# Wider attention products, paired LayerNorm statistics and single-copy normalised tiles in a vision tower on one core

## The chip, the cores and the metric

The kernel runs on one core of a Trainium2 chip. The metric is device time in microseconds (us) from start to end of one execution, and the median of several executions counts. The core has five engines with queues of their own: TensorE (PE, with its weight loads shown apart as PEld), VectorE (DVE), ScalarE (ACT), GpSimd (POOL) and SyncE (SP), which only issues transfers. They meet through semaphores.

## The reference

1,024 tokens of 192 features go through five blocks; all of it is computed in one launch.

1. Tokenizer: 960 pixel values per token, LayerNorm, a product to 192 features.
2. Masked attention, 12 heads of 16 features, 64 sequences of 16 tokens: `out = softmax(q k^T / 4 + mask) v`, projected and added.
3. A mixture of 8 experts of 288 hidden units, the two best kept for each token.
4. A block of the RWKV kind: two LayerNorms in a row, a recurrence forward and backward, an output product, a second normalised feed-forward part (768 units, squared ReLU) with a gate.
5. Attention again, with a gated low-rank addition to q, k and v from 8 experts.

Each of the five phases starts with `(x - mean(x)) * rsqrt(var(x) + eps)` over the 192 features of each token.

## The kernel before

**Layout.** Tokens lie in 8 tiles of 128 (token on the partition). The residual stream is `H` (128 x 8 x 192, float32), the stream inside block 4 is `Z`. Products need features on the partitions, so each normalised tile is written to `xn` and turned by TensorE into a PSUM bank. ACT then writes the float16 high part `X_hi` and DVE the remainder `X_lo` (`x_low`), and every product of the kernel is made of float16 high and low parts. Features 128 to 191 are needed twice, at partitions 0 to 63 and again at 64 to 127.

**LayerNorm of one tile** (`ln_stats`, line 1010; `one_over_std`, line 505; `ln_norm`, line 1016). DVE runs `bn_stats` (line 1011), waits for it by a semaphore, runs `bn_aggr` (line 1012). POOL adds epsilon (line 508), waits for itself, and raises to the power -0.5 (line 511). DVE writes `xn` in two instructions: 192 columns (line 1021), then columns 128 to 191 a second time beside them (line 1024). TensorE turns the 256 columns with two float32 transposes per tile (`turn`, line 1572), two tiles to a bank, and the last one releases ACT.

**The order of LayerNorm work.** `norm_tiles` (line 1032) handles four tiles: statistics of tile t, then `ln_norm` of tile t-1, so each tile's root runs on POOL while DVE works on the next tile. It is called six times: tiles 0 to 3 and 4 to 7 before the experts (`moe`), before the feed-forward part of block 4 (`mix2`), and before the second attention (`attn1`). Block 4's two LayerNorms in a row are `norm_twice` (line 1045), with a root for H, a normalisation to Z (line 1053), and a root for Z per tile. Tiles 0 to 3 of it are spread over expert steps 9 to 14; tiles 4 to 7 come in one piece when the experts are done. The first attention's tiles (`attn0`) call `ln_stats` and `ln_norm` one by one in the tokenizer's loop (lines 1299 to 1308).

**Attention** (`attention`, lines 724, 1091, 1609). Two halves of 512 tokens, hf 0 and 1, are interleaved by a list of steps, `ATTENTION_ORDER`: ... `pt` 0, `ot` 0, `st` 1, `pj` 0, `values0` 1, `s` 1, `values1` 1, `pt` 1, `ot` 1, `pj` 1. `st` (`scores`, line 1630) forms for each of 32 groups of 16 tokens (g) a product of a block-diagonal key matrix (made by DVE's `spread`, line 1108) with 16 tokens' queries: for high and low parts one product of 2 x 16 columns and one of 16, times two row sets of 128 and 64 features. That is 128 products a half, in 4 banks. `ot` (`outputs`, line 1694) does the same with values and probabilities. DVE sums each bank's two column sets (line 1143). `pj` is the output projection, 24 products of 192 columns. `values0/1` are 128 float16 transposes a half which ACT (lines 732, 738) and DVE (line 1139) copy out. `s` and `pt` turn scores and probabilities.

**Planned banks.** Every use of a PSUM bank is planned in `plan_fills`: it names the previous user whose release TensorE waits for. SP issues the next weight transfer when POOL has finished the low parts (`low_part`, line 513) of the weights before.

## Time and profile before

| | |
|---|---|
| median of 3 runs | 509.55 us (505.12, 509.55, 509.74) |
| the profiled execution | 506.86 us, span 505.1 us |
| mean granted TensorE clock | 0.78 of full speed |
| PE / PEld busy | 344.7 us (68%) / 257.1 us (51%) |
| DVE busy | 412.2 us (82%), 896 instructions |
| ACT / POOL busy | 227.3 us (45%) / 144.7 us (29%) |
| tokenizer | 0 to 62 us |
| first attention | 62 to 150 us |
| experts | 144 to 250 us |
| block 4: double LayerNorm, recurrence, feed-forward | 250 to 394 us |
| second attention with its gates | 389 to 505 us |

Busy time says how long an engine held an instruction, not whether anyone waited for it. The chain of waits follows the last instruction back to what released it, so it names the engine that set the time in each stretch. A granted clock of 1.00 is 2.4 GHz, 0.50 is 1.2 GHz.

### The profile page before, as it was taken

The numbers are of one execution on the slowest core, as the hardware profiler recorded it, in microseconds if no ns is written. First come the engines' busy times: TensorE is split into PE (matmuls) and PEld (weight loads), VectorE is DVE, ScalarE is ACT, GpSimd is POOL, SyncE is SP. The second block draws the span as 40 slices with busy tenths as digits, with TensorE's granted clock in tenths as the row PEclk, the third lists the DMA queues.
The fourth block names the chain that finished last, engine by engine and source line by source line (L and its number), as shares of the span: only waits on it lengthen the run. The fifth ranks groups of instructions, "written<-read, shape, count | busy, mean of one in ns | idle before, by whom it ended". The sixth has DMA issues, their size and how long they took to land.

```text
span 505.1 us, 8830 instructions
## 1 busy us (share of the span) xinstructions
PE 344.7 (68%) x3474; PEld 257.1 (51%) x3474; DVE 412.2 (82%) x896; ACT 227.3 (45%) x391; POOL 144.7 (29%) x194
## 2 busy tenths in 40 slices
PE   4766649897769899999926000006799268798976
PEld 4665619596646567776702000004359125655955
DVE  3799998998886654887779999998899869776974
ACT  4566383718375796644315660000084122363171
POOL 3535252042430433242042469811301120000000
PEclk9979986959577999999968555555599668578586
DMA  7635000030050002000000000000000000000000
GB/s 275 228 106 228 2 1 1 1 143 1 2 215 1 2 0 95 2 1 1 0 2 1 0 0 0 0 1 0 2 0 1 1 1 1 1 2 1 2 34 31
DMA packets 4235, 17.51 MB, mean 35 GB/s; under 512 B 857, under 2 KB 1762, under 8 KB 3682
## 3 DMA queue, kind: packets, MB, share of 16 engines
q1 hardware_dynamic: 4194, 16.95, 9.2%
q8 instruction: 27, 0.44, 0.4%
q14 instruction: 14, 0.11, 0.1%
HBM read 16.16 MB, written 0.79 MB: 34 GB/s over the span
## 4 chain that ended last, share of the span: by engine, by line
DVE 46%; PE 34%; ACT 8%; issue 6%; POOL 4%; DMA 1%; SPq 0%; DVEq 0%; POOLq 0%; ACTq 0%
PE PS L1527 30%; DVE R L1108 4%; DVE R L1378 3%; DVE R L1380 3%; POOL rstd L511 3%; DVE R L1432 2%; DVE Q L1098 2%; PE PS L1659 2%; DVE R L1001 1%; DVE stats L1011 1%; DMA T<-tok_w 1%; DVE xn L1021 1%; DVE stats L964 1%; POOL ve L508 1%; PE PS L1666 1%
## 5 line engine op out<-in xcount | busy, mean ns | idle before, releaser
L1527 PE MATMUL PS<-late_a,Q 128*128 128x192 f16 x48 | 9.9, 360 | 72.0 <-DVE Q L1435 70.3
L508 POOL TENSOR_SCALAR ve<-mv 128x1 f32<-128x1 f32 x56 | 14.4, 257 | 149.9 <-DVE mv L1012 131.1
L1527 PE MATMUL PS<-Q,R 128*128 128x32 f16 (+3 forms) x1024 | 46.4, 192 | 14.0 <-DVE R L1108 9.7
L1527 PE MATMUL PS<-m,Q 128*128 128x192 f16 (+1 forms) x576 | 51.9, 245 | 2.4 <-DVE Q L1324 2.4
L1527 PEld LDWEIGHTS PS<-Q,R 64*64 64x64 f16 (+1 forms) x1024 | 44.6, 125 | 17.2 <-DVE R L1108 10.2
L1527 PEld LDWEIGHTS PS<-m,Q 128*128 128x128 f16 (+1 forms) x576 | 45.8, 96 | 11.8 <-issue 8.0
L1527 PEld LDWEIGHTS PS<-late_a,Q 128*128 128x128 f16 x48 | 6.2, 139 | 73.8 <-issue 73.4
L1324 DVE TENSOR_TENSOR Q<-Q 128x512 f16<-128x512 f32 x36 | 26.5, 751 | 19.2 <-ACT Q L813 19.0
L1527 PE MATMUL PS<-X_hi,R 128*128 128x512 f16 x144 | 41.2, 392 | 0.0
L808 ACT ACTIVATE Q<-PS,col 128x512 f32<-128x512 f32 x36 | 24.8, 689 | 28.9 <-PE PS L1527 28.8
L1108 DVE TENSOR_SCALAR R<-Q,K 128x1024 f16<-128x1024 f16 x80 | 37.3, 539 | 0.3
L1527 PE MATMUL PS<-X_hi,late_a 128*128 128x512 f16 (+1 forms) x72 | 30.4, 445 | 10.1 <-DVE X_hi L1088 5.6
L511 POOL TENSOR_TENSOR rstd<-ve,mhalf 128x1 f32<-128x1 f32 x56 | 33.6, 600 | 4.7
L1339 DVE SCALAR_TENSOR_TENSOR H<-PS,gat,H 128x192 f32<-128x192 f32 x64 | 23.2, 411 | 5.8 <-PE PS L1527 4.8
L1582 PE MATMUL PS<-K,xn 128*128 128x128 f32 x80 | 16.3, 324 | 13.6 <-DVE xn L1024 13.5
L1527 PE MATMUL PS<-R 128*128 128x192 f16 x184 | 17.8, 257 | 10.8 <-DVE R L981 10.8
L1527 PE MATMUL PS<-X_hi,late_b 128*128 128x512 f16 (+1 forms) x72 | 25.2, 431 | 0.0
L813 ACT ACTIVATE Q<-PS,col 128x512 f16<-128x512 f32 x36 | 24.9, 690 | 0.0
L732 ACT ACTIVATE R<-PS 128x1024 f16<-128x1024 f16 x16 | 15.6, 1015 | 19.7 <-PE PS L1659 19.7
L1143 DVE TENSOR_REDUCE Q<-PS 128x128 f32<-128x256 f32 x64 | 22.1, 408 | 2.8 <-PE PS L1527 2.7
L516 POOL TENSOR_TENSOR R<-T,R 128x576 f16<-128x576 f32 x8 | 15.7, 1989 | 26.7 <-ACT T L712 26.7
L1527 PEld LDWEIGHTS PS<-X_hi,R 128*128 128x128 f16 x144 | 14.4, 100 | 16.5 <-issue 2.2
(233 smaller groups left out, 932.3 us busy)
## 6 DMA issues: line engine op xcount, KB each, us to landing
R<-tok_x SPq DMA_DIRECT2D x8, 480.0 KB, 3.6
T<-tok_w SPq DMA_DIRECT2D x6, 480.0 KB, 7.3
T<-late SPq DMA_DIRECT2D x1, 2632.0 KB, 8.7
T<-moe SPq DMA_DIRECT2D x1, 2304.0 KB, 8.8
T<-moe SPq DMA_DIRECT2D x1, 1728.0 KB, 8.0
T<-full SPq DMA_DIRECT2D x1, 1152.0 KB, 5.3
R<-early SPq DMA_DIRECT2D x1, 776.0 KB, 9.8
out<-H SPq DMA_DIRECT2D x4, 192.0 KB, 1.9
```

The costliest lines, as they stand in the source:

```text
L508: nc.gpsimd.tensor_scalar(ve[:, t:t + 1], mv[:, t, 1:2], EPS, None, ALU.add).then_inc(pool_step, 1)
L511: nc.gpsimd.tensor_tensor(rstd[:, t:t + 1], ve[:, t:t + 1], mhalf[:], ALU.pow).then_inc(rstd_ready, 1)
L516: nc.gpsimd.tensor_tensor(lo, raw, hi, ALU.subtract).then_inc(wlo, 1)
L732: nc.scalar.activation(VA[:, hl, 8 * g:8 * g + 8, :], bank(name).bitcast(F16).rearrange("p (s n) -> p s n", s=8), ACT.Copy).then_inc(v_act ...
L808: nc.scalar.activation(ge[n % 3], bank(("h", n)), ACT.Gelu, bias=b, scale=1.0 / WS).then_inc(act_step, 1)
L813: nc.scalar.activation(hgh[slot], bank(("h", n)), ACT.Gelu, bias=b, scale=1.0 / WS).then_inc(gelu_ready, 1)
L1108: ins = V.tensor_scalar(v[:, :, :, h], w, K[:, mask + h:mask + h + 1], None, ALU.mult)
L1143: return V.tensor_reduce(dst, src.rearrange("p (l n) -> p n l", l=2), AX, ALU.add)
L1324: V.tensor_tensor(hgl[slot], ge[n % 3], hgh[slot], ALU.subtract).then_inc(hp_ready, 1)
L1339: ins = V.scalar_tensor_tensor(H[:, t], bank(name)[:, C * j:C * j + C], gat[:, 5, t, e:e + 1], H[:, t], ALU.mult, ALU.add)
L1527: return T_.matmul(o, w, x, start=start, stop=stop, skip_group_check=True)
L1582: last = T_.transpose(bank(name)[:, 256 * j + P * k:256 * j + P * k + P], xn[:, t % 4, P * k:P * k + P], ident)
```

## The change

LayerNorm statistics are taken for two tiles at a time and POOL raises a 128 x 2 operand instead of 128 x 1; in `norm_tiles` both pairs' statistics come first and the four normalisations after them; `norm_twice` spreads as pairs over the same six steps. The first attention's tiles keep `ln_stats`. `xn` holds 192 columns, written once; each tile is turned by a transpose of columns 0 to 127 and one of columns 64 to 191, and columns 128 to 191 are turned a third time into partitions 0 to 63 of the second, over the part of it that is not wanted. In `st` of half 1 and `ot` of half 0, group s writes up to 3 groups of 16 columns (times 2 for high and low) in its first product and up to 6 in its second. The columns beyond its own 16 are overwritten by the next group, whose first product starts afresh. `ot` of half 1 and `st` of half 0 keep their 32 and 16 columns.

```diff
@@ -502,13 +502,13 @@
             nc.gpsimd.memset(ones[:], 1.0).then_inc(const_ready, 1)
             steps = [0]
 
-            def one_over_std(n, t):
+            def one_over_std(n, t, w=1):
 
                 pool.wait_ge(var_ready, n + 1)
-                nc.gpsimd.tensor_scalar(ve[:, t:t + 1], mv[:, t, 1:2], EPS, None, ALU.add).then_inc(pool_step, 1)
+                nc.gpsimd.tensor_scalar(ve[:, t:t + w], mv[:, t:t + w, 1], EPS, None, ALU.add).then_inc(pool_step, 1)
                 steps[0] += 1
                 pool.wait_ge(pool_step, steps[0])
-                nc.gpsimd.tensor_tensor(rstd[:, t:t + 1], ve[:, t:t + 1], mhalf[:], ALU.pow).then_inc(rstd_ready, 1)
+                nc.gpsimd.tensor_tensor(rstd[:, t:t + w], ve[:, t:t + w], mhalf[:, 0:w], ALU.pow).then_inc(rstd_ready, 1)
 
             def low_part(n, raw, hi, lo):
 
@@ -578,12 +578,9 @@
             pool.wait_ge(wlo, NM + NL + 1)
 
             for hf in range(2):
-                for k in range(5):
-                    if k:
-                        one_over_std(n, 4 * hf + k - 1)
-                        n += 1
-                    if k < 4:
-                        one_over_std(n, 4 * hf + k)
+                for _ in ("H", "Z"):
+                    for t in (4 * hf, 4 * hf + 2):
+                        one_over_std(n, t, 2)
                         n += 1
 
             def link(ins):
@@ -1013,15 +1010,22 @@
                 nn[0] += 1
                 return nn[0]
 
+            def ln_stats_pair(t, src):
+                c = 6 * (t // 2 % 2)
+                sa, sc = stats[:, 0, c:c + 6], stats[:, 1, c:c + 6]
+                V.bn_stats(sa, src[:, t])
+                link(V.bn_stats(sc, src[:, t + 1]))
+                V.bn_aggr(mv[:, t], sa)
+                V.bn_aggr(mv[:, t + 1], sc).then_inc(var_ready, 1)
+                nn[0] += 1
+                return nn[0]
+
             def ln_norm(t, src, n, k):
 
                 dve.wait_ge(rstd_ready, n)
                 if k >= 4:
                     dve.wait_ge(psum_filled, x_fill(k - 4))
-                V.tensor_scalar(xn[:, t % 4, 0:C], src[:, t], mv[:, t, 0:1], rstd[:, t:t + 1], ALU.subtract,
-                                ALU.mult).then_inc(dve_step, 1)
-                chain[0] += 1
-                V.tensor_scalar(xn[:, t % 4, C:2 * P], src[:, t, P:C], mv[:, t, 0:1], rstd[:, t:t + 1], ALU.subtract,
+                V.tensor_scalar(xn[:, t % 4], src[:, t], mv[:, t, 0:1], rstd[:, t:t + 1], ALU.subtract,
                                 ALU.mult).then_inc(xn_ready, 1)
 
             def x_fill(k):
@@ -1031,29 +1035,30 @@
 
             def norm_tiles(src, ready=None, tiles=range(NT)):
 
-                last = None
-                for t in range(tiles[0], tiles[-1] + 2):
-                    if t in tiles:
-                        if ready:
-                            ready(t)
-                        now = ln_stats(t, src)
-                    if last:
-                        ln_norm(t - 1, src, last, xc[0])
+                seen = []
+                for t in range(tiles[0], tiles[-1], 2):
+                    if ready:
+                        ready(t)
+                    seen.append(ln_stats_pair(t, src))
+                for t in tiles:
+                    ln_norm(t, src, seen[(t - tiles[0]) // 2], xc[0])
+                    xc[0] += 1
+
+            def norm_twice(hf, k):
+
+                t = 4 * hf + 2 * (k % 2)
+                if k < 2:
+                    first[t] = ln_stats_pair(t, H)
+                elif k < 4:
+                    dve.wait_ge(rstd_ready, first[t])
+                    V.tensor_scalar(Z[:, t], H[:, t], mv[:, t, 0:1], rstd[:, t:t + 1], ALU.subtract, ALU.mult)
+                    link(V.tensor_scalar(Z[:, t + 1], H[:, t + 1], mv[:, t + 1, 0:1], rstd[:, t + 1:t + 2],
+                                         ALU.subtract, ALU.mult))
+                    second[t] = ln_stats_pair(t, Z)
+                else:
+                    for i in range(2):
+                        ln_norm(t + i, Z, second[t], xc[0])
                         xc[0] += 1
-                    last = now
-
-            def norm_twice(hf, k):
-
-                if k >= 2:
-                    ln_norm(4 * hf + k - 2, Z, second[k - 2], xc[0])
-                    xc[0] += 1
-                if 1 <= k < 5:
-                    t = 4 * hf + k - 1
-                    dve.wait_ge(rstd_ready, first[k - 1])
-                    link(V.tensor_scalar(Z[:, t], H[:, t], mv[:, t, 0:1], rstd[:, t:t + 1], ALU.subtract, ALU.mult))
-                    second[k - 1] = ln_stats(t, Z)
-                if k < 4:
-                    first[k] = ln_stats(4 * hf + k, H)
             first, second = {}, {}
 
             def x_low(phase, pairs_=range(4)):
@@ -1574,13 +1579,15 @@
                 for pr in pairs_:
                     name = ("x", phase, pr)
                     free(name)
+                    x = xn[:, 2 * pr % 4:2 * pr % 4 + 2]
+                    o = bank(name).rearrange("p (j k n) -> p j k n", j=2, k=2)
                     for j in range(2):
                         xc[0] += 1
                         pe.wait_ge(xn_ready, xc[0])
-                        t = 2 * pr + j
-                        for k in range(2):
-                            last = T_.transpose(bank(name)[:, 256 * j + P * k:256 * j + P * k + P],
-                                                xn[:, t % 4, P * k:P * k + P], ident)
+                        T_.transpose(o[:, j, 0], x[:, j, 0:P], ident)
+                        T_.transpose(o[:, j, 1], x[:, j, CB:C], ident)
+                    for j in range(2):
+                        last = T_.transpose(o[0:CB, j, 1], x[:, j, P:C], ident)
                     last.then_inc(psum_filled, 1)
 
             def by_rows(o, wa, wb, col0, m, hf, more=()):
@@ -1627,26 +1634,33 @@
                             more = ((bh, hw_hi[:, sl]), (bh, hw_lo[:, sl]), (bl, hw_hi[:, sl]), (bb, cstack[0:72, sl]))
                         by_rows(bank(name)[0:m], wa, wb, c0 + o, m, hf, more).then_inc(psum_filled, 1)
 
+                def columns(g, s, images):
+                    n = 16 * min(images, 8 - s)
+                    return slice(16 * g, 16 * g + n), slice(16 * s, 16 * s + n)
+
                 def scores(hf):
 
                     n0 = 2 * a + hf
                     pe.wait_ge(bd_ready, 3 * n0 + 2)
                     pe.wait_ge(qkv_ready, 5 * n0 + 5)
                     qa, qb = pairs["QA"], pairs["QB"]
+                    near, far = (3, 6) if hf == 1 else (1, 1)
                     for t in range(4):
                         name = ("st", a, hf, t)
                         free(name)
                         oa, ob = (bank(name)[:, 2 * P * k:2 * P * (k + 1)].rearrange("p (l n) -> p l n", l=2) for k in range(2))
                         for s in range(8):
                             g = 8 * t + s
-                            q, o = slice(16 * g, 16 * g + 16), slice(16 * s, 16 * s + 16)
+                            q, o = columns(g, s, near)
+                            ql, ol = columns(g, s, far)
                             mm(oa[:, :, o], KAbd[:, 0, g], qa[:, :, q], True, False)
-                            mm(oa[:, 0, o], KAbd[:, 1, g], qa[:, 0, q], False, True)
+                            mm(oa[:, 0, ol], KAbd[:, 1, g], qa[:, 0, ql], False, True)
                         for s in range(8):
                             g = 8 * t + s
-                            q, o = slice(16 * g, 16 * g + 16), slice(16 * s, 16 * s + 16)
+                            q, o = columns(g, s, near)
+                            ql, ol = columns(g, s, far)
                             mm(ob[0:CB, :, o], KVBbd[0:CB, 0, g], qb[0:CB, :, q], True, False)
-                            last = mm(ob[0:CB, 0, o], KVBbd[0:CB, 1, g], qb[0:CB, 0, q], False, True)
+                            last = mm(ob[0:CB, 0, ol], KVBbd[0:CB, 1, g], qb[0:CB, 0, ql], False, True)
                         last.then_inc(psum_filled, 1)
 
                 def values(hf, hl):
...
```

(POOL's other calls of `one_over_std` go over even tiles with width 2 in the same way; `outputs` gets the same edit as `scores`, with `columns(s, s, near)` on the probabilities and `near, far = (3, 6) if hf == 0 else (1, 1)`; `mhalf` grows from [P, 1] to [P, 2], `xn` from [P, 4, 256] to [P, 4, 192].)

## Rows read from the trace of the kernel before

**Rows 1.** The page's chain that ended last, by engine
```profile
DVE 46%; PE 34%; ACT 8%; issue 6%; POOL 4%; DMA 1%; SPq 0%; DVEq 0%; POOLq 0%; ACTq 0%
```

**Rows 2.** Windows: stretch, then busy us (and instructions) of each engine, granted clock, DMA
```profile
50.00:60.00 10.00, 5.84 (x65) 5.44 (x64) 9.60 (x28) 4.06 (x7) 2.90 (x8) 1.00 0.00 1
170.00:244.00 74.00, 72.76 (x619) 52.13 (x619) 49.97 (x119) 46.54 (x81) 24.20 (x29) 1.00 0.05 17
```

**Rows 3.** Timeline of DVE, one norm_tiles call: start us, duration us, instruction, [idle before]
```profile
389.15 0.36 DVE L1011 BATCH_NORM_STATS2 stats<-H 128x6 f32<-128x192 f32 x1
389.54 0.18 DVE L1012 BATCH_NORM_AGGREGATE mv<-stats 128x2 f32<-128x6 f32 x1
389.64 0.33 DVE L1011 BATCH_NORM_STATS2 stats<-H 128x6 f32<-128x192 f32 x1
...
390.72 0.38 DVE L1021 TENSOR_SCALAR xn<-H,mv,rstd 128x192 f32<-128x192 f32 x1 [0.54 <-POOL rstd L511]
391.02 0.31 DVE L1024 TENSOR_SCALAR xn<-H,mv,rstd 128x64 f32<-128x64 f32 x1
391.24 0.35 DVE L1011 BATCH_NORM_STATS2 stats<-H 128x6 f32<-128x192 f32 x1
...
394.31 0.55 DVE L1473 SCALAR_TENSOR_TENSOR R<-R,PS 128x384 f32<-128x384 f32 x1
```

**Rows 4.** Timeline of POOL beside it, the first two roots
```profile
389.81 0.22 POOL L508 TENSOR_SCALAR ve<-mv 128x1 f32<-128x1 f32 x1 [24.76 <-DVE mv L1012]
390.12 0.57 POOL L511 TENSOR_TENSOR rstd<-ve,mhalf 128x1 f32<-128x1 f32 x1
390.66 0.22 POOL L508 TENSOR_SCALAR ve<-mv 128x1 f32<-128x1 f32 x1
```

**Rows 5.** Timeline of POOL and DVE, the end of the experts' first norm_tiles
```profile
133.67 2.52 POOL L516 TENSOR_TENSOR m<-T,m 128x576 f16<-128x576 f32 x2
...
133.74 1.32 DVE L1021 TENSOR_SCALAR xn<-H,mv,rstd 128x192 f32<-128x192 f32 x1 [0.34 <-POOL rstd L511]
134.99 1.26 DVE L1024 TENSOR_SCALAR xn<-H,mv,rstd 128x64 f32<-128x64 f32 x1
```

**Rows 6.** Timeline of DVE, first instruction of norm_twice and the first behind it
```profile
250.10 0.36 DVE L1011 BATCH_NORM_STATS2 stats<-H 128x6 f32<-128x192 f32 x1
...
262.70 0.54 DVE L1076 TENSOR_SCALAR R<-PS,col 128x256 f32<-128x256 f32 x1
```

**Rows 7.** Timeline of PE: transposes at either clock, products of 192 columns
```profile
353.81 1.80 PE L1582 MATMUL PS<-K,xn 128*128 128x128 f32 x6
355.80 0.69 PE L1582 MATMUL PS<-K,xn 128*128 128x128 f32 x2 [0.19 <-DVE xn L1024]
...
365.42 1.04 PE L1582 MATMUL PS<-K,xn 128*128 128x128 f32 x8
...
385.61 6.10 PE L1527 MATMUL PS<-fullp,R 128*128 128x192 f16 x72
```

**Rows 8.** Timeline of DVE, two waits behind a norm_tiles call
```profile
366.06 0.55 DVE L1076 TENSOR_SCALAR R<-PS,col 128x256 f32<-128x256 f32 x1 [0.37 <-PE PS L1582]
...
418.26 0.75 DVE L1098 SCALAR_TENSOR_TENSOR Q<-PS,col,Q 128x512 f16<-128x512 f32 x1 [0.82 <-ACT Q L752]
```

**Rows 9.** Timeline of PE: st of half 1, first attention; ot and st, second
```profile
105.04 5.99 PE L1527 MATMUL PS<-Q,R 128*128 128x32 f16 x128 [0.17 <-DVE R L1108]
...
462.92 11.49 PE L1527 MATMUL PS<-Q,R 128*128 128x32 f16 x256 [1.28 <-DVE Q L1163]
```

**Rows 10.** Windows of line 1527 alone in ot and st: PE, PEld, clock, DMA
```profile
99.72:101.72 2.00, 2.00 (x62) 1.93 (x63) 1.00 0.00 0
...
470.00:472.00 2.00, 2.00 (x50) 1.93 (x50) 0.50 0.03 8
```

**Rows 11.** Timeline of DVE: the softmax of half 1, first and second attention
```profile
119.12 0.56 DVE L1118 SCALAR_TENSOR_TENSOR Q<-PS,K 128x384 f32<-128x384 f32 x1 [1.52 <-PE PS L1677]
...
481.75 0.56 DVE L1121 TENSOR_SCALAR Q<-PS 128x384 f32<-128x384 f32 x1 [0.72 <-PE PS L1677]
```

More of the change, by code:

```diff
@@ L250, in build @@
         id16 = sb("id16", [P, P], F16)
-        mhalf = sb("mhalf", [P, 1])
+        mhalf = sb("mhalf", [P, 2])
         tokb = sb("tokb", [P, C])
@@ L258, in build @@
         rstd = sb("rstd", [P, NT])
-        xn = sb("xn", [P, NT // 2, 2 * P])
+        xn = sb("xn", [P, NT // 2, C])
         X_hi = sb("X_hi", [P, NT, 2, P], F16)
@@ L564, in _ @@
                 if i == 11:
-                    for t in range(4):
-                        one_over_std(n, t)
+                    for t in (0, 2):
+                        one_over_std(n, t, 2)
                         n += 1
                 low_part(i, raw, hi, lo)
-            for t in range(4, NT):
-                one_over_std(n, t)
+            for t in (4, 6):
+                one_over_std(n, t, 2)
                 n += 1
@@ L580, in _ @@
             for hf in range(2):
-                for k in range(5):
-                    if k:
-                        one_over_std(n, 4 * hf + k - 1)
-                        n += 1
-                    if k < 4:
-                        one_over_std(n, 4 * hf + k)
+                for _ in ("H", "Z"):
+                    for t in (4 * hf, 4 * hf + 2):
+                        one_over_std(n, t, 2)
                         n += 1
@@ L629, in _ @@
             for phase in range(2):
-                for t in range(NT):
-                    one_over_std(n, t)
+                for t in range(0, NT, 2):
+                    one_over_std(n, t, 2)
                     n += 1
@@ L1697, in outputs @@
                     pe.wait_ge(v_dve_ready, 4 * (n0 + 1))
+                    near, far = (3, 6) if hf == 0 else (1, 1)
                     for t in range(4):
@@ L1704, in outputs @@
                             g = 8 * t + s
-                            q = o = slice(16 * s, 16 * s + 16)
+                            q, o = columns(s, s, near)
+                            ql, ol = columns(s, s, far)
                             mm(oa[:, :, o], VA[:, 0, g], PT[:, :, t, 0, q], True, False)
-                            mm(oa[:, 0, o], VA[:, 1, g], PT[:, 0, t, 0, q], False, True)
+                            mm(oa[:, 0, ol], VA[:, 1, g], PT[:, 0, t, 0, ql], False, True)
                         for s in range(8):
                             g = 8 * t + s
-                            q = o = slice(16 * s, 16 * s + 16)
+                            q, o = columns(s, s, near)
+                            ql, ol = columns(s, s, far)
                             mm(ob[0:CB, :, o], VB[0:CB, 0, g], PT[0:CB, :, t, 1, q], True, False)
-                            last = mm(ob[0:CB, 0, o], VB[0:CB, 1, g], PT[0:CB, 0, t, 1, q], False, True)
+                            last = mm(ob[0:CB, 0, ol], VB[0:CB, 1, g], PT[0:CB, 0, t, 1, ql], False, True)
                         last.then_inc(psum_filled, 1)
```

## The prediction

> **What bounds the kernel.** I read the chain of waits first: DVE sets the end for 46% of the span and PE for 34%, POOL alone for 4% [rows 1]. So no engine is the bound throughout, and each edit has to be priced in its own stretch. The windows say which: in the tokenizer DVE works 96% of the time; in the 74 us of the experts PE works 98% at full clock with DVE at 50 of 74 us [rows 2], so LayerNorm work there costs nothing unless it lies on PE. The timelines of the LayerNorm calls come next. One call for four tiles takes 389.15 to 394.31 = 5.16 us on DVE, with waits for POOL's root in it, and nothing else is on DVE meanwhile [rows 3]. The double LayerNorm of block 4 takes 12.60 us for four tiles [rows 6]. Last, the attention: st of half 1 waits only for DVE's spread at 105.04 [rows 9], and DVE waits behind it for 1.52 us in the first attention and 0.72 in the second [rows 11]. That wait bounds what faster products can give.
>
> **LayerNorm, one call of four tiles.** From the rows: bn_aggr starts 0.39 us after its bn_stats, the next bn_stats 0.10 later; a 192-column xn write takes 0.30 start to start, the second write 0.22 [rows 3]. POOL's epsilon starts 0.27 after bn_aggr, the root 0.31 later, the root takes 0.57, and the next epsilon may start 0.03 before it ends [rows 4]. DVE starts 0.03 after the root. I take 0.26 for two bn_stats in a row (0.33 less the overlap seen between unlinked instructions). New call, from zero: bn_stats 0 and 0.26, bn_aggr 0.65 and 0.75, second pair 0.85 to 1.60; first root 1.33 to 1.90; second epsilon 1.87, root 2.18 to 2.75; xn at 1.94, 2.24, 2.78, 3.08, next work at 3.38. That is 5.16 - 3.38 = 1.78 us less a call, of which 4 x 0.22 are the dropped writes and the rest waits.
>
> **The root of two columns** is nowhere in the trace. It isn't cheaper than one (0.57), and at most it is double (1.14). Between them I take 0.75: of the 0.57, 0.22 is what the plain epsilon takes [rows 4] and only the remaining 0.35 can grow, which caps it near 0.92; 0.75 is the middle. Then the call ends at 3.74 and saves 1.42 us (at 1.14: it ends at 4.52 and saves 0.64).
>
> **Which calls are on the path.** Six calls:
> - Experts, tiles 0 to 3: DVE goes straight on. Two xn writes run into POOL's weight low parts and take 1.32 and 1.26 us instead of 0.38 and 0.31 [rows 5]. POOL again starts these as soon as its last root is out, so I keep the collision: two writes meet it, as before. Saves 1.4.
> - Experts, tiles 4 to 7: x_low behind it waits for the last transposes, which now are four after the last xn instead of two. At full clock a transpose is (1.04 - 0.27)/7 = 0.11 us [rows 7], so 0.2 is given back. Saves 1.2.
> - mix2, tiles 0 to 3: PE works at half clock there, and pair 0's transposes can't start before the output products end at 353.81. A transpose costs 0.69 - 0.48 = 0.21 us at that clock [rows 7]; twelve instead of eight add 0.8, which eats what the earlier xn gives. Mix2, tiles 4 to 7: DVE already waits 0.37 us for PE's transposes, which stand behind three key products [rows 8]. The xn come 1.4 us earlier for nothing and four transposes more cost 0.4. Both together: -0.4.
> - attn1, tiles 0 to 3: the feed-forward output of tiles 4 to 7 is ready on PE at 391.7, before DVE gets to it. Saves 1.4.
> - attn1, tiles 4 to 7: after it DVE waits 0.82 us for ACT and PE's second qkv slot [rows 8]; PE is the limit. The wait grows by what the call gives. 0.
>
> **The double LayerNorm, tiles 4 to 7.** Same steps: both pairs of H statistics 0 to 1.78; roots ready at 2.08 and 3.11; Z of pair 0, its statistics to about 3.8; Z of pair 1, its statistics to about 5.3; roots of Z out at 4.8 and 6.4; last xn at about 6.8, next work at 7.1. x_affine of pair 1 then waits some 0.35 for four transposes at half clock. 12.60 - 7.45 = **5.15 us** (5.5 at 0.57, 4.1 at 1.14). It is the largest term: per tile a root of H and a root of Z were waited for one after the other, four times; now it is twice each with the other pair between. All of it is on the path, since nothing else runs on DVE and the recurrence behind it needs the same engine.
>
> **Tokenizer.** Eight second writes of 0.22 go; DVE has 96% there, ACT sometimes ends the wait. I count 1.5 of the 1.76. **Transposes inside the experts:** the mix1 turn sits in PE's full stretch; four more x 0.11 = 0.4 lost. Elsewhere the extra transposes lie in PE's idle time.
>
> **The 96-column products.** What the rows show: at full clock a 24-column product (mean of 32 and 16) comes every 2.00/62 = 32 ns, at half clock every 2.00/50 = 40 (45 over the whole 256, which take 11.49 us) [rows 9, 10]. PE is busy throughout both windows, and yet the clock, 1.00 in the first two us of `ot`, is 0.50 well inside it. 72 products of 192 columns take (6.10 - 0.17)/72 = 82 ns each [rows 7], that is 2.4 columns per ns plus 2.4 ns, and 619 such wide instructions hold 1.00 for 74 us [rows 2]. The new products have 96 columns down to 16 at the end of each bank: mean 75. At full clock, by the larger of 32 ns and columns/2.4 + 3, that is 39 ns each, 5.0 us a half-step instead of 5.2 to 6.0; at half clock 65 ns, 8.3 us. I take the full clock: streaming then fills 0.8 of the time, against 0.3 now, nearer to the rows that hold it than to those that lose it. Gain, first attention: st starts at 105.04 with the spread as before [rows 9], ends at 110.0 instead of 111.0, and the 24 products of the projection run at full clock, 2 us instead of 4. PE is then 3 us ahead and the value transposes wait for DVE's spread, so the gain is at most DVE's 1.52 us wait [rows 11]. ACT, which copies values out and weights before them without a pause, passes on about half: 0.85. In the second attention ACT has no weights to split; there DVE's 0.72 goes whole [rows 11], with two pauses of 0.15 ahead of it: 1.05. The 0.85 goes unchanged into the experts' first call, since there DVE follows at once. Together 1.9.
>
> The Trainium skill (TensorE: Matmul & The Clock Gate, section Back-to-back issue gap) says that a stream of weight load and matmul pairs settles at about 81 ns a product at 128 columns. The trace disagrees: 82 ns is its figure for 192 columns, not for 128 [rows 7]. By the page 256 products would take an estimated 20.7 us and the kernel would end near 515, where the last rival ends too.
>
> **Sum.** 1.5 + 1.4 + 1.2 - 0.4 (mix1 turn) + 5.15 - 0.4 (mix2) + 1.4 + 1.9 = 11.75 us. From the profiled execution of 506.86: 495.1. The median before is 2.7 above the profile, and two of three runs lie there; by it, 497.8. I say **496**. With the root at 0.57 it is 1.5 less, with 1.14 it is 3.4 more.
>
> **Rivals.**
> 1. *The root of two costs twice one.* 0.57 to 1.14: 506.86 - 8.4 = 498.5. For it: 0.35 of the 0.57 is work beyond an add.
> 2. *The gain comes back in a queue.* PE or ACT stands behind one of the calls I count in full, as it does in mix2; with attn1 and one experts' call gone and half of the attention's 1.9: 506.86 - 8 = 499 to 501. For it: PE is busy in every stretch after a call but one.
> 3. *The clock falls all the same.* Full clock for the first 2 us, then 65 ns each: 51 products in the 2 us and 205 x 0.065 = 13.3 make 15.3 us for 256, against 11.3 now (5.2 + 6.0 in the first attention, 11.5 in the second), in both attentions. That is 8 lost instead of 1.9 won: 506.86 - 9.85 + 8 = 505, within 1%. Against it: the fill of 0.8.
> 4. *Slower: each wide product takes about 80 ns*, as 96 columns would at half clock throughout with nothing overlapped. 256 of them take 20.5 us instead of 11.3, in both attentions, and DVE waits for all of it: +18.2 - 9.85 gives 515. It decides from (11.3 + 9.85/2) us for 256, or 63 ns each, upward. Against it: 82 ns at 192 columns [rows 7].
>
> **Chances.** The forecast 0.72, rival 1 0.08, rival 2 0.08, rival 3 0.08, rival 4 0.04. A measurement of this kernel tells about 1% (5 us) from nothing. Rivals 1 and 2 are faster by more than that except for some 0.02; with rival 3 that makes 0.10 for within 1%, 0.04 slower, 0.86 faster. Range: the low end is the root at 0.57 and both mix2 and the second attn1 call giving 1.5 each, 506.86 - 16 = 491; the high end takes in rivals 1 and 2 on the basis of the median, 502.
>
> **What would show it.** In the page after: granted clock 1.00 or near in `ot` 0 and `st` 1, 39 ns a product; no L1024 group; 36 roots on POOL instead of 56; the root's mean, 0.57 to 1.14; each LayerNorm call 3.4 to 3.8 us; double LayerNorm near 7; in mix2 longer waits of DVE for PE. I am wrong if the two-column root is above 1.2 us, if the clock is 0.5 in the wide products, or if DVE's new waits behind the calls sum to more than 5 us.

## The result, and the profile after

| | before | after |
|---|---|---|
| median | 508.07 us (505.12 to 509.74, 20 runs) | 502.39 us (494.00 to 505.06, 20 runs) |
| profiled execution, span | 506.86, 505.1 | 504.28, 502.4 |
| PE / DVE / POOL busy | 344.7 / 412.2 / 144.7 us | 358.6 / 399.7 / 129.7 us |
| DVE instructions | 896 | 856 |
| mean granted clock | 0.78 | 0.784 |

The executions of the changed kernel fall into two groups: 9 of 20 at 494.0 to 497.4 us, with a mean clock of 0.80 to 0.81, and 11 at 502.4 to 505.1, at 0.78. The kernel before has one group. The comparison leaves out runs that lie over 1.5% above the fastest of their kernel (here and in every ratio below), so its ratio of 0.9756 (95% interval 0.9732 to 0.9779) is that of the lower group; the medians of all runs stand as 0.989, a gain of 5.7 us. The forecast of 496 is the lower group (mean 495.4), the mean of the upper is 503.7, and the profile shown here is one of the upper group. So there are two questions: do the steps hold, and what are the 8 us between the groups?

The chain of waits by engine in the page after, beside [rows 1]: DVE and POOL, where the LayerNorm part works, have less, PE 6 points more.

```profile
DVE 41%; PE 40%; ACT 9%; issue 6%; POOL 2%; DMA 1%; SPq 0%; DVEq 0%; POOLq 0%; ACTq 0%
```

**LayerNorm.** DVE's timeline of the call that [rows 3] show (start us, duration us, instruction, idle before and releaser):

```profile
388.31 0.36 DVE L1016 BATCH_NORM_STATS2 stats<-H 128x6 f32<-128x192 f32 x1
...
390.35 0.67 DVE L1028 TENSOR_SCALAR xn<-H,mv,rstd 128x192 f32<-128x192 f32 x2 [0.35 <-POOL rstd L511]
391.34 0.67 DVE L1028 TENSOR_SCALAR xn<-H,mv,rstd 128x192 f32<-128x192 f32 x2 [0.32 <-POOL rstd L511]
391.92 0.55 DVE L1478 SCALAR_TENSOR_TENSOR R<-R,PS 128x384 f32<-128x384 f32 x1
```

From the first bn_stats to the next work it is 3.61 us (forecast 3.74, before 5.16). What remains are two waits for POOL, one a pair. On POOL the root of two columns takes 0.71 us, and the next pair's epsilon starts before it ends:

```profile
256.28 0.22 POOL L508 TENSOR_SCALAR ve<-mv 128x2 f32<-128x2 f32 x1 [20.08 <-DVE mv L1019]
256.59 0.71 POOL L511 TENSOR_TENSOR rstd<-ve,mhalf 128x2 f32<-128x2 f32 x1
257.27 0.22 POOL L508 TENSOR_SCALAR ve<-mv 128x2 f32<-128x2 f32 x1
```

The double LayerNorm of tiles 4 to 7, DVE, beside [rows 6]: 255.30 to 262.18 = 6.88 us, with 0.50 of a new wait for PE's transposes behind it (forecast 7.1 and 0.35, before 12.60).

```profile
255.30 0.36 DVE L1016 BATCH_NORM_STATS2 stats<-H 128x6 f32<-128x192 f32 x1
...
260.34 0.64 DVE L1028 TENSOR_SCALAR xn<-T,mv,rstd 128x192 f32<-128x192 f32 x2
261.60 0.67 DVE L1028 TENSOR_SCALAR xn<-T,mv,rstd 128x192 f32<-128x192 f32 x2 [0.61 <-POOL rstd L511]
262.18 0.54 DVE L1081 TENSOR_SCALAR R<-PS,col 128x256 f32<-128x256 f32 x1
...
263.67 0.54 DVE L1081 TENSOR_SCALAR R<-PS,col 128x256 f32<-128x256 f32 x1 [0.50 <-PE PS L1590]
```

**The wide products.** PE's timeline of `ot` 0 and `st` 1, 256 products in one row, in the first and the second attention; [rows 9] have the narrow ones. Then PE's windows in the first (stretch, length, PE busy and instructions, granted clock, DMA share and GB/s):

```profile
100.88 18.47 PE L1532 MATMUL PS<-Q,R 128*128 128x96 f16 x256 [2.11 <-DVE Q L1168]
...
460.39 10.99 PE L1532 MATMUL PS<-Q,R 128*128 128x96 f16 x256 [1.28 <-DVE Q L1168]
```

```profile
100.00:101.00 1.00, 0.12 (x3) 1.00 0.00 0
101.00:102.00 1.00, 1.00 (x18) 0.53 0.00 0
102.00:103.00 1.00, 1.00 (x16) 0.50 0.00 0
...
118.00:119.00 1.00, 1.00 (x18) 0.50 0.00 0
...
122.00:123.00 1.00, 1.00 (x19) 1.00 0.00 0
```

The same 256 products take 18.47 us in the first attention and 10.99 in the second. In the first the clock is 1.00 while TensorE waits 2.11 us, and 0.50 right after it starts to work. It stays at 0.50 for 20 us in which PE is busy without a pause, and comes back 2.3 us into the 192-column products behind them. The difference, 7.5 us, is near the 8.3 us between the means of the two groups.

**The ledger by stretch**, each from the start of one instruction of the timelines to the start of the next named, the last one DVE's last residual add; "filled" is the run f1_fill below, whose first attention holds the clock.

| stretch (us) | before | after | filled | forecast gain |
|---|---|---|---|---|
| to the first low part of qkv (tokenizer) | 64.63 | 64.67 | 64.79 | 1.5 |
| to `st` 0 | 11.55 | 12.05 | 12.05 | 0 |
| to `ot` 0 | 23.54 | 24.16 | 23.75 | 0 |
| `ot` 0 and `st` 1, to `pj` 0 | 11.24 | 18.40 | 10.94 | } 0.85 |
| to `ot` 1 | 17.19 | 15.85 | 15.96 | } |
| to the experts' ct transposes (two calls) | 37.44 | 33.89 | 33.94 | 2.6 |
| experts, to the first b2 product | 37.65 | 39.41 | 39.42 | 0 |
| to the last b2 product (mix1 turn) | 44.07 | 44.52 | 44.52 | -0.4 |
| double LayerNorm, to the recurrence | 18.99 | 13.41 | 13.42 | 5.15 |
| recurrence and mix2, to feed-forward | 103.35 | 102.46 | 102.46 | -0.4 |
| to the second attention's gates | 30.68 | 29.11 | 29.09 | 1.4 |
| to `ot` 0 of the second attention | 62.59 | 62.46 | 62.44 | 0 |
| to the last residual add | 39.27 | 39.09 | 39.09 | 1.05 |

The columns after and filled differ by 7.6 us, 7.46 of it in one line.

### The profile page after: what moved, and what is told of

The parts are those of the page before. It is cut to its first block, busy times and chain, and to the rows that moved or that the text cites. A ratio compares the mean times of both kernels' runs of the same rounds, so it can differ in the third digit from the quotient of the medians.

```text
span 502.4 us, 8830 instructions
## 1 busy us (share of the span) xinstructions
PE 358.6 (71%) x3514; PEld 272.6 (54%) x3514; DVE 399.7 (80%) x856; ACT 227.7 (45%) x391; POOL 129.7 (26%) x154
## 4 chain that ended last, share of the span: by engine, by line
DVE 41%; PE 40%; ACT 9%; issue 6%; POOL 2%; DMA 1%; SPq 0%; DVEq 0%; POOLq 0%; ACTq 0%
PE PS L1532 34%; DVE R L1383 3%; DVE R L1385 3%; DVE R L1113 3%; DVE R L1437 2%; DVE Q L1103 2%; PE PS L1673 2%; DVE R L998 1%; DMA T<-tok_w 1%; POOL rstd L511 1%; PE PS L1680 1%; DVE stats L961 1%; ACT Q L886 1%; DVE R L1397 1%; DVE smx L1128 1%
## 5 line engine op out<-in xcount | busy, mean ns | idle before, releaser
L1532 PE MATMUL PS<-Q,R 128*128 128x96 f16 (+9 forms) x1024 | 52.0, 208 | 13.1 <-DVE R L1113 8.9
L1532 PEld LDWEIGHTS PS<-Q,R 64*64 64x64 f16 (+1 forms) x1024 | 50.3, 124 | 16.3 <-DVE R L1113 9.3
L1532 PE MATMUL PS<-m,Q 128*128 128x192 f16 (+1 forms) x576 | 53.5, 249 | 3.0 <-ACT Q L822 2.4
L1532 PEld LDWEIGHTS PS<-m,Q 128*128 128x128 f16 (+1 forms) x576 | 47.2, 98 | 12.3 <-issue 6.9
L508 POOL TENSOR_SCALAR ve<-mv 128x2 f32<-128x2 f32 (+1 forms) x36 | 8.6, 238 | 160.9 <-DVE mv L1019 133.4
L1532 PE MATMUL PS<-X_hi,R 128*128 128x512 f16 x144 | 39.6, 380 | 0.0
L1532 PE MATMUL PS<-R 128*128 128x192 f16 x184 | 20.6, 280 | 8.5 <-DVE R L978 8.5
L511 POOL TENSOR_TENSOR rstd<-ve,mhalf 128x2 f32<-128x2 f32 (+1 forms) x36 | 24.3, 675 | 3.0
L1532 PEld LDWEIGHTS PS<-R 128*128 128x128 f16 x184 | 18.3, 112 | 10.1 <-DVE R L978 9.7
L862 ACT ACTIVATE Q<-R 128x512 f16<-128x512 f32 x3 | 1.9, 629 | 46.4 <-DVE R L1438 46.4
## 6 DMA issues: line engine op xcount, KB each, us to landing
R<-early SPq DMA_DIRECT2D x1, 776.0 KB, 10.3
```

The costliest lines, as they stand in the source:

```text
L511: nc.gpsimd.tensor_tensor(rstd[:, t:t + w], ve[:, t:t + w], mhalf[:, 0:w], ALU.pow).then_inc(rstd_ready, 1)
L1532: return T_.matmul(o, w, x, start=start, stop=stop, skip_group_check=True)
```

## The experiments

Twelve kernels, in three sets of four; those of a set ran on one chip beside the kernel before, most of them 6 times (e3 8, g1 12). Theory A: the wide products keep a full clock that they find and don't bring back a lost one, and the 2.1 us idle ahead of `ot` 0 is where it is lost. Theory B: the groups come from elsewhere.

**Which part makes the groups.** Four runs: the changed kernel again; its LayerNorm part alone; the wide products alone on the kernel before; everything, with wide products in the second attention only.

```diff
 e2_ln_only (both places):
-                    near, far = (3, 6) if hf == 1 else (1, 1)
+                    near, far = 1, 1
 e4_wide_second:
+                    near, far = (3, 6) if a == 1 and hf == 1 else (1, 1)
```

> The changed kernel once more, unchanged. In its profile the clock stood at 0.50 through `ot` 0 and `st` 1 of the first attention (256 products in 18.5 us) and at 1.00 in the second attention. Theory A: wide products keep a full clock that they find, but don't bring one back; whether they find it after PE's 2.1 us of idle ahead of `ot` 0 differs from execution to execution. Then executions fall into two groups some 8 us apart, near 495 and 503, and a profile of the lower group shows about 10 us for the 256 products. Theory B: the two groups come from another stretch (tokenizer, experts), and the 256 products take about 18 us in both.

> The LayerNorm part alone (pairs, single copy, three transposes); all attention products narrow as in the kernel before. Theory A: one group of executions, 8 to 10 us under the kernel before (ratio 0.981 to 0.984), by the LayerNorm terms read from the profile of after: about 1.5, 1, 5.1, 0.9, 1.5 us. Theory B: two groups 8 us apart here too.

> The kernel before with the wide products alone. Theory A: two groups, one about 2 us under the kernel before (as forecast: 0.85 + 1.05), one some 5 to 7 us above it. Theory B: one group, within 2 us of the kernel before.

> The changed kernel with wide products in the second attention only; the first attention's are narrow. Theory A: the slow group is gone; all executions lie at 496 to 498, since the second attention held its clock in the profile of after, and its gain of 1 us stays. Theory B: still two groups 8 us apart.

| | median us (range) | ratio to before, 95% |
|---|---|---|
| before | 507.49 | |
| e1_after_again | 503.35 (495.1; five at 502.5 to 504.4) | 0.983, 0.976 to 0.990 |
| e2_ln_only | 499.75 (498.2 to 504.5) | 0.986, 0.983 to 0.990 |
| e3_wide_only | 510.16 (508.9 to 511.2, one 515.0) | 1.006, 1.004 to 1.009 |
| e4_wide_second | 499.44 (495.7 to 501.2) | 0.983, 0.979 to 0.987 |

Without wide products in the first attention (e2, e4) nothing lies above 501.2 but one run of 504.5; with them (e1) five of six do. So the groups seem to come with the wide products of the first attention. The LayerNorm part gives 7.7 us in the median, a little less than the 8 to 10 expected, and e4 lies above the 496 to 498 expected. The profile of e4 shows something more: narrow products, and the clock lost at their start all the same.

```profile
98.36 11.89 PE L1532 MATMUL PS<-Q,R 128*128 128x32 f16 x256 [2.11 <-DVE Q L1168]
```

```profile
99.00:100.00 1.00, 1.00 (x22) 0.50 0.00 0
```

From `ot` 0 to `pj` 0 it needs 11.8 us, and the kernel before, which loses the clock only within `ot` 0, 11.2. So the loss needs no wide products, and with narrow ones it costs 0.6 us instead of 7.5. But e3 goes against the simple form of A and fits neither of its two groups: with the same wait of 2.11 us ahead of it, its stream holds the full clock, and yet the kernel is slower than before. First PE's `ot` 0 of e3, then its windows in the experts:

```profile
99.13 10.99 PE L1527 MATMUL PS<-Q,R 128*128 128x96 f16 x256 [2.11 <-DVE Q L1163]
```

```profile
166.00:168.00 2.00, 1.40 (x7) 1.00 0.01 4
168.00:170.00 2.00, 0.15 (x2) 0.99 0.00 0
170.00:172.00 2.00, 2.00 (x14) 0.50 0.00 0
172.00:174.00 2.00, 2.00 (x15) 0.50 0.00 0
...
176.00:178.00 2.00, 2.00 (x9) 0.80 0.05 8
```

It gains 1.3 us from `ot` 0 to `ot` 1 and loses 3.3 in the experts, behind another wait of TensorE (2.45 us, ahead of the down products of unit 3), and 1.2 in the second attention ahead of `ot` 0. The experts' loss is not a matter of the change: their first stretch took 37.65 us in the profile of before and 39.3 to 40.9 in the five others so far, always behind that wait. An idle of 2 us or more is thus survived at times and not at others.

**Fill the idle.** Added products of 512 columns write a PSUM bank that is free and overwritten later: nine ahead of `ot` 0 (f1), ten more ahead of the experts' unit 3 (f2), and the nine with narrow products throughout (f3).

```diff
+                        if a == 0 and hf == 0 and t == 0:
+                            for _ in range(9):
+                                mm(bank(name), id16[:], wa[:, 0, 0:512], True, True)
                         pe.wait_ge(pt_ready, 2 * n0 + t // 2 + 1)
 f2_fill_both, besides:
+                    if u == 3:
+                        spare = ("h", unit_chunks(u + 1)[0][0])
+                        free(spare)
+                        for _ in range(10):
+                            mm(bank(spare), id16[:], early_a[:, 0, 0:512], True, True)
                     free(("y", v, 0))
```

> The kernel after, with nine added products of 512 columns on TensorE (0.22 us each at full clock, about 1.95 us) that write the still unused PSUM bank of the first `ot` tile, in the 2.1 us in which TensorE waits for VectorE's last pt copy ahead of `ot` 0 of the first attention. Their result is overwritten; nothing else changes. Theory A (the 96-column products keep a full clock they find and do not bring one back; the idle ahead of `ot` 0 is what takes it): the first attention's 256 products take 10.9 us at granted clock 1.00 in every execution, the upper group of times (502 to 505) is gone, and the median lies at 494 to 497. Theory B (the two groups come from elsewhere, or the clock falls by what came earlier): both groups stay and the products still take 18.4 us in the upper one; median 502 to 504. If the added products themselves are late, ot 0 starts later by up to 0.3 us.

> The kernel of the run before (nine added products ahead of `ot` 0) and ten more added products of 512 columns ahead of the down products of the experts' unit 3, where TensorE waits 2.45 us in every profile so far, after which the clock was 1.00 in one profile and 0.50 for 3 to 7 us in the five others. They write the PSUM bank of the next unit's first chunk, which is free there. Theory A: the clock stays at 1.00 in the experts, and the stretch from the ct transposes to the b2 products takes 37.7 us instead of 39.4: 1.5 us under the run before, 493 to 495. Theory B (the clock there does not follow from that idle): no change, or up to 1 us slower where the added products end after the wait.

> The nine added products ahead of `ot` 0, but all attention products 16 and 32 columns wide as in the kernel before (the LayerNorm part of the change stays). If the narrow stream loses the clock by itself, `ot` of the first attention starts at 1.00 and falls to 0.50 within it, as in the profile of before, and the time is that of the kernel with the LayerNorm part alone, 498 to 500. If only the idle ahead of it took the clock, 256 products take 8.2 us (32 ns each) and the time is that of the wide kernel with the added products, 494 to 497: then the width is not needed.

With the kernel before at 508.03: f1 496.38 us (495.1 to 496.7 four times, 500.7 and 501.0), ratio 0.980 (0.976 to 0.984); f2 **491.71** (489.8 to 495.5), ratio 0.971 (0.967 to 0.975); f3 499.23 (495.6 to 505.6), ratio 0.981 (0.978 to 0.984). PE of f1, then of f3:

```profile
98.41 2.11 PE L1532 MATMUL PS<-early_a,id 128*128 128x512 f16 x9
100.59 11.00 PE L1532 MATMUL PS<-Q,R 128*128 128x96 f16 x256
```

```profile
95.94 2.11 PE L1532 MATMUL PS<-early_a,id 128*128 128x512 f16 x9
98.12 4.79 PE L1532 MATMUL PS<-Q,R 128*128 128x32 f16 x128
103.53 5.99 PE L1532 MATMUL PS<-Q,R 128*128 128x32 f16 x128 [0.61 <-DVE R L1113]
```

```profile
98.00:100.00 2.00, 1.93 (x58) 1.00 0.00 0
100.00:102.00 2.00, 2.00 (x62) 0.92 0.03 8
102.00:104.00 2.00, 1.39 (x32) 0.50 0.00 0
```

In f1 the added products end just before the first product of `ot` 0 starts, and 256 wide products take 11.0 us instead of 18.5. In f1, f2 and g4 below, 18 runs, none lies above 501.0 and 16 lie under 497; of the 32 runs of the changed kernel in three sets 21 lie at 501.3 to 505.1. That idle is what costs the upper group its clock. (Some 5 us are lost in some other place as well, which no profile shows: f1 has two runs at 500.7 and 501.0, f2 three at 493.3 to 495.5 beside three at 489.8 to 490.1, and f3, without wide products, two at 505.1 and 505.6, at a mean clock of 0.77 and not the 0.78 of the changed kernel's upper group. So a run's time alone doesn't say which loss it had.) In f3 the narrow stream has the same full clock ahead of it and falls to 0.50 within 4 us: the wide stream keeps a clock that the narrow one loses, as the prediction had it. What that is worth in time is not settled: the medians differ by 2.9 us, with ranges that overlap, but in f3's profile, the fastest of its six, the stretch from `ot` 0 to the ct transposes takes 61.2 us, in f1's 60.8, in e2's (narrow, idle not filled) 63.4. And with ten products in the experts' wait, the stretch to the first b2 product takes 37.75 us instead of 39.4, at 1.00 throughout. PE's windows there, of the changed kernel and of f2:

```profile
174.00:176.00 2.00, 1.22 (x14) 1.00 0.00 0
176.00:178.00 2.00, 2.00 (x16) 0.54 0.04 8
178.00:180.00 2.00, 2.00 (x14) 0.61 0.00 0
```

```profile
164.00:166.00 2.00, 1.72 (x12) 1.00 0.00 0
166.00:168.00 2.00, 2.00 (x26) 1.00 0.03 8
172.00:174.00 2.00, 2.00 (x24) 1.00 0.00 0
```

Over all profiles: 37.6 to 37.8 us in the three kernels with those ten products (f2, g1, g4), 37.65 in one of the eleven without them, 39.3 to 40.9 in ten. The median of f2 lies 4.7 us under that of f1 and under the 493 expected at the lowest, which these 1.7 us don't account for. In its profile 2.3 us more are gained in the second attention ahead of `ot` 0 (60.1 against 62.4) and 1.5 in the tokenizer, where nothing was added; g4, with the same ten products, has 62.4 there.

**Do the added products pay by themselves?** Both stretches of them in the kernel before.

> The kernel BEFORE, with none of the change, and both stretches of added products (nine ahead of `ot` 0 of the first attention, ten ahead of the down products of the experts' unit 3). If the added products are worth something by themselves, whatever the change, it is 1.5 us or more under the kernel before. By theory A they need the wide products to pay in the attention: the narrow stream loses the clock within itself (in the run with added products and narrow columns it fell 3 us in), and in the experts the profile of before showed no loss to win back. So within 1 us of before in its profile, and 0 to 2 us in the median, by how often the experts' clock falls.

506.94 us (12 runs) against 507.55 (17 runs), ratio 1.000 (0.998 to 1.002). They don't. In g1's profile the clock is 1.00 ahead of its narrow products and falls to 0.78 and 0.50 within 4 us of their start, as in f3. What the added products give, they give to the wide stream and to the experts.

**The single write and third transposes.** Undone in f4: two writes and two transposes a tile, as before.

```diff
...
+                V.tensor_scalar(xn[:, t % 4, C:2 * P], src[:, t, P:C], mv[:, t, 0:1], rstd[:, t:t + 1], ALU.subtract,
...
 turn():
+                        for k in range(2):
+                            last = T_.transpose(bank(name)[:, 256 * j + P * k:256 * j + P * k + P],
+                                                xn[:, t % 4, P * k:P * k + P], ident)
```

> The kernel after with the third part of the change undone: each normalised tile is written twice by VectorE (192 columns and the last 64 again) and transposed twice by TensorE instead of written once and transposed three times; pairs with one root each and the 96-column products stay. By the prediction the single write saves 0.22 us a tile where VectorE sets the end (8 tiles of the tokenizer, 4 and 4 of the experts, 4 of the double LayerNorm, 4 of attn1) and the third transpose costs 0.4 us at mix1 and 0.4 at mix2: 24 x 0.22 = 5.3, of which some 1.5 was lost in the tokenizer's clock, less 0.8: 3 to 4.5 us slower than the kernel after in the same group of times, which for the upper group is 506 to 508. The rival that the third transposes eat the gain says no difference (within 1 us).

498.29 us (494.5, 495.7, 496.7, 499.9, 500.9, and 507.7), ratio 0.980 (0.976 to 0.984). Its profile is 500.87, 4.2 above f1's, of which 1.4 is the experts' clock. In the double LayerNorm it needs only 0.27 us more (13.69 against 13.42), where four second writes of 0.22 had been counted. DVE there shows why:

```profile
256.50 0.31 DVE L1031 TENSOR_SCALAR xn<-T,mv,rstd 128x64 f32<-128x64 f32 x1
256.97 0.38 DVE L1028 TENSOR_SCALAR xn<-T,mv,rstd 128x192 f32<-128x192 f32 x1 [0.16 <-POOL rstd L511]
...
258.92 0.53 DVE L1084 TENSOR_SCALAR R<-PS,col 128x256 f32<-128x256 f32 x1
```

The first pair's second writes lie in the wait for the root (0.16 instead of 0.61), and nothing is waited for behind the call, where the third transposes cost 0.50. Against them stand 0.5 us ahead of `st` 0 and 0.44 at mix1, which f4 gets back. Five runs of 494.5 to 500.9 have a mean of 497.5, against 495.4 for the nine of the changed kernel's lower group, but 497.6 for the six of f1, which holds the clock in the same place. So the part is worth 0 to 2 us, not the 3 to 4.5 expected; these few runs don't tell it from nothing. One thing I had not looked for: by their times, 12 of 14 runs with two writes (e3 and f4) are without the 7.5 us, and 15 of 38 with one write (after, e1, g2, g3). The profiles with wide products and the idle left as it is agree, two of two and none of four. The wait is 2.1 us in both, and why the number of writes should matter is not shown.

**Columns and a lost clock; a third place filled.** g2 is the changed kernel once more, g3 has (4, 8) for (3, 6), g4 is f2 with added products ahead of `pt` 1 and `ot` 1 and wide products in `ot` 1 of the first attention too.

```diff
 g4_fill_three, in the turn of the probabilities:
+                        if a == 0 and hf == 1:
+                            for _ in range(1 if pr else 9):
+                                mm(bank(name), id16[:], wa[:, 0, 0:512], True, True)
...
 and in ot:
+                    near, far = (3, 6) if hf == 0 or a == 0 else (1, 1)
```

> The kernel after once more, beside the versions with added products on the same chip. Both theories: two groups of times, 494 to 498 and 502 to 505; theory A says that the version with both stretches of added products (490 to 495.5) lies under both groups.

> The kernel after with 128 columns instead of 96 in the wide products (four images in both parts instead of three, eight instead of six). At full clock 256 of them take (mean 104 columns) 104 / 2.4 + 3 = 46 ns each = 11.9 us, 1 us more than now; the lower group is then 0 to 1 us above that of the kernel after. If more columns bring a lost clock back, the upper group is gone. By theory A (what is lost ahead of `ot` stays lost until the 192-column products of the projection) they run at half clock throughout where it is lost, some 95 ns each = 24 us, and the upper group lies near 508 to 511.

> The version with both stretches of added products, and more of them: nine ahead of the transposes of the probabilities of half 1 of the first attention (TensorE waits 2.3 us there), one and two in the waits behind these, and 96-column products in `ot` of half 1 as well. Now those 256 products run at half clock and narrow, about 11.5 us, and the projection behind them at half clock, 4 us. Theory A: the clock holds, they take 11 us and the projection 2 us; the gain is at most 2.5 us, less what VectorE, which stands behind `ot` here, takes anyway: 0 to 2 us under the version before it, 488 to 494. If the clock falls all the same, 96 columns at half clock cost 18.4 us instead of 11.5: 5 to 7 us slower than it, 496 to 501.

Beside 507.55 for before: g2 502.96 us (495.7; five at 501.3 to 504.3), ratio 0.985 (0.979 to 0.990). g3 497.43 (four at 494.4 to 498.2, two at 506.5 and 506.7, under the 508 to 511 expected), ratio 0.977 (0.974 to 0.981). g4 493.78 (491.9 to 496.6), ratio 0.973 (0.970 to 0.976). PE of g3 in the first and second attention:

```profile
100.30 21.38 PE L1532 MATMUL PS<-Q,R 128*128 128x128 f16 x256 [2.11 <-DVE Q L1168]
...
462.77 12.38 PE L1532 MATMUL PS<-Q,R 128*128 128x128 f16 x256 [1.28 <-DVE Q L1168]
```

128 columns don't bring the clock back either: 0.50 for 21 us. (The expectation put their mean at 104; over both products of a group it is 88, hence 48 ns each at full clock and 84 at half.) g4 can't be told from f2 by the intervals, and the gain of 0 to 2 us expected over it isn't there. Its stretch of `ot` 1 held the clock, but the wait for VectorE behind it grew from 1.41 us in f2 to 2.70, and after the next one the clock was 0.50, where f2 had 1.00:

```profile
125.38 5.54 PE L1532 MATMUL PS<-Q,R 128*128 128x96 f16 x128 [0.43 <-DVE Q L1168]
...
135.08 0.41 PE L1532 MATMUL PS<-early_a,Q 128*128 128x192 f16 x3 [2.70 <-DVE Q L1183]
145.91 0.19 PE L1532 MATMUL PS<-early_a,X_hi 128*128 128x8 f16 x1 [1.94 <-DVE X_hi L1070]
```

```profile
144.00:146.00 2.00, 0.09 (x3) 0.93 0.52 215
146.00:148.00 2.00, 2.00 (x50) 0.50 0.00 0
```

From `ot` 1 to the ct transposes it needs 35.1 us, f2 33.9. So f2 has the lowest median of all: 16.3 us under the kernel before (508.03 to 491.71), in part by the stretches named above that nothing was added to.

## Why the prediction was right or wrong

The forecast of 496 lies in the lower group, but only 9 of 20 runs are there, and the number is met in part by luck. With the clock held in the first attention (f1's profile) the stretches gain 10.3 us for the 11.75 of the sum: the tokenizer, the two stretches behind it, the experts and the second attention give 5.0 less than forecast; the first attention with the experts' calls, the double LayerNorm and mix2 give 3.3 more. The prediction's own sign of being wrong, a clock of 0.5 in the wide products, came in the other runs.

- **One call of four tiles: right.** 3.61 us for 3.74. The root of two columns took 0.71 us, near the 0.75 taken between 0.57 and 1.14, so rival 1 is out. The collision with POOL's low parts [rows 5] came as forecast: 5.54 us from 136.08 to 141.62 instead of 7.06, with one pair of writes caught.

```profile
138.11 0.67 DVE L1028 TENSOR_SCALAR xn<-H,mv,rstd 128x192 f32<-128x192 f32 x2 [0.36 <-POOL rstd L511]
139.12 2.57 DVE L1028 TENSOR_SCALAR xn<-H,mv,rstd 128x192 f32<-128x192 f32 x2 [0.34 <-POOL rstd L511]
```

- **Double LayerNorm: right**, 5.6 us for 5.15. Which part gave it was said less well: f4 shows that pairs give nearly all, the dropped writes 0.27.
- **Experts' calls and the first wide part: right in direction** where the clock holds. Filled against before, from `ot` 0 to the ct transposes: 65.87 - 60.84 = 5.0 us for 3.45. Of these the LayerNorm part alone gives 2.5 (e2), and the other 2.5 are not all the wide products': the narrow f3 has 2.2 of them. So the 0.85 of the wide products lies between the 0.4 and the 2.5 that the profiles leave for them. The changed kernel, in its upper group, has -2.3 there.
- **mix1 turn and attn1: right.** -0.45 for -0.4, 1.57 for 1.4, and 0.1 for 0: DVE's waits for ACT behind that call grew, as said [rows 8].

```profile
414.19 0.75 DVE L1103 SCALAR_TENSOR_TENSOR Q<-PS,col,Q 128x512 f16<-128x512 f32 x1 [1.36 <-ACT Q L749]
416.99 0.75 DVE L1103 SCALAR_TENSOR_TENSOR Q<-PS,col,Q 128x512 f16<-128x512 f32 x1 [2.05 <-ACT Q L749]
```

- **mix2: too low.** The new waits for the transposes are there (1.36 and 0.28 at 355 us, 1.11 at 365), but the stretch gained 0.9 instead of losing 0.4. In the profiles of e2, e4 and g4, with the same LayerNorm code, it gained 0.1 to 0.2. The difference of 0.8 between executions is larger than the term.
- **Tokenizer, 1.5 us: not seen.** 64.67 for 64.63, and 0.5 more than before up to `st` 0, where a third transpose stands in a stretch that I had called idle. The first mark lies at 62.1 to 64.8 us in the ten profiles with one write and at 63.4 to 65.3 in the four with two. Their means, 63.5 and 64.3, leave room for 0.8; with such a spread it can't be settled.
- **"I take the full clock": the step that failed.** The wide stream does keep the clock (f1 at 1.00, where f3 and g1 fall to 0.50); that its fill of 0.8 is the reason no run shows, and it is silent on whether the clock is there at the start. I priced the products by what they do to the clock and not by what TensorE did before them. The row was at hand in the trace of the kernel before, where the clock passed:

```profile
99.72 5.16 PE L1527 MATMUL PS<-Q,R 128*128 128x32 f16 x128 [2.11 <-DVE Q L1163]
```

  For narrow products a lost clock costs little (11.8 us from `ot` 0 to `pj` 0 in e4 instead of 11.2, where the clock falls within `ot` 0), for wide ones 18.4 instead of 10.9. So the change raised the price of an event that already could happen, and 7.5 us came back in 21 of 32 runs. Rival 3 had the mechanism half right: half clock from the first product and not after 2 us, 18.4 us for 256 and not 15.3, in the first attention only. Its price for the whole kernel, 505, is the top of the upper group by luck: it charged 4 us in each of two attentions, where 7.5 fell in one.
- **39 ns a wide product: 4 ns low.** 10.99 us for 256 is 43 ns, and at half clock 72 instead of 65. Rival 4 (80 ns throughout) did not come. The Trainium skill (TensorE: Matmul & The Clock Gate, section Back-to-back issue gap) gives columns / 2.4 + 2.5 ns for matmuls alone; for a mean of 75 columns that is an estimated 34 ns, and the trace has 9 more.
- **Experts' own clock: not in the sum.** 1.76 us lost behind a wait that the change doesn't touch, and the profile of before was the one that happened not to lose them. A forecast made from one profile inherits its luck.
- **Second attention, 1.05 us: 0.2 seen** against before, 0.9 against the LayerNorm part alone (39.09 and 39.97 in e2). DVE's wait of 0.72 for PE [rows 11] is gone, but one of 0.50 for PE comes just ahead of it, so that DVE is 0.46 earlier at the copies of the probabilities, and 0.28 of that is lost behind them: the last two waits for the projection are 1.38 and 1.36 us instead of 1.37 and 1.07.

```profile
477.56 1.29 DVE L1144 COPY R<-PS 128x1024 f16<-128x1024 f16 x2 [0.50 <-PE PS L1691]
...
499.48 0.56 DVE L1191 SCALAR_TENSOR_TENSOR H<-PS,H 128x384 f32<-128x384 f32 x1 [1.36 <-PE PS L1532]
```

What decides whether the 2.1 us idle takes the clock is open. By their times it did in 21 of 32 runs of the changed kernel, in 2 of 6 of g3, in 2 of 14 with two writes. In the five profiles where it did (after, e1, g2, g3 and, with narrow products, e4) the clock fell within 0.3 us of the first product, before or behind it; in e3 and f4 it never fell in the stream. So it is decided about where the stream starts, whatever its width, and filling the idle ends it; the runs don't show why the same idle passes in one execution and not in the next.

## What to carry to other kernels

Before you widen or lengthen a stream on TensorE to hold its clock, look at what the engine does just ahead of it: a wait of 2 us there made the stream's clock a matter of the execution here, and the wide stream paid 7.5 us for what cost the narrow one 0.6. Filling that wait with products into a free bank cost nothing here, as they end before the awaited operand comes (ratio 1.000 in g1), and it pays only with a stream behind it that can hold the clock. Statistics and roots taken for two tiles at a time paid most where two LayerNorms follow each other with nothing beside them, and a median alone can hide that a kernel has two times.

## What was not expected of the hardware

- A stream with PE busy in every microsecond ran at clock 0.50 for 18 us (96 columns) and 21 us (128 columns), while the same stream holds 1.00 for 11 us when it starts there. In the changed kernel's profile the 192-column products behind it had the clock back after 2.3 us.
- The same wait of 2.45 us in the experts was followed by 1.00 in one profile and by 3 to 7 us at 0.50 in ten.
- A root of two columns on GpSimd costs 0.71 us, one column 0.57.
